# The setup of a gated cross-attention kernel: constant matmuls during the first loads, a smaller first load, another order of keys, queries and mask words

## The reference, cut to what matters

```python
x = x + tanh(g_xattn[0]) * xattn(layernorm(x), ctx_1024, mask, Wq, Wk, Wv, Wo)   # 2048 rows of 256
x = x + tanh(g_ffn[0])   * ffn(layernorm(x), Wg, W1, W2, W3)                     # 8 experts, 2 for each row

def xattn(inputs_q, inputs_kv, mask, Wq, Wk, Wv, Wo):        # 16 heads of 64, 1601 keys
    q = inputs_q @ Wq; k = inputs_kv @ Wk; v = inputs_kv @ Wv
    scores = einsum('bthd,bThd->bhtT', q, k) / sqrt(64)
    scores = where(mask, scores, finfo(float32).min)
    return (softmax(scores) @ v) @ Wo
```

## Time and profile before

| | |
|---|---|
| median of 3 runs | 627.38 us (626.77 to 627.91) |
| profiled execution | 626.95 us, span 625.1 us, so 1.85 us lie around the span |
| TensorE (PE) matmul busy | 590.8 us, 95% |
| VectorE (DVE) busy | 406.8 us, 65% |
| GpSimd (POOL) busy | 309.0 us, 49% |
| ScalarE (ACT) busy | 272.5 us, 44% |
| mean granted TensorE clock | 0.990 of full speed |

### The profile page before, as it was taken

The page is one execution under the profiler, slowest core; times in us unless marked ns, Lnnn a source line. Parts: engine busy times, 40 slices in busy tenths (PEclk is TensorE's granted clock), DMA queues, the critical chain, the costliest instruction groups (busy, mean ns, idle before and its releaser), DMA issues.

```text
span 625.1 us, 10907 instructions
## 1 busy us (share of the span) xinstructions
PE 590.8 (95%) x2882; PEld 343.7 (55%) x2883; DVE 406.8 (65%) x1266; ACT 272.5 (44%) x713; POOL 309.0 (49%) x272
## 2 busy tenths in 40 slices
PE   3899999999999999999999999889999999999993
PEld 2444465555556555555655555446666656666562
DVE  3578978898998989988899976247353222322231
ACT  2765665566565665665655554212412221122210
POOL 3643554565564698565796655412463222222221
PEclk9999999999999999999999989989999999999998
DMA  8944577586777889687686866999576442333312
GB/s 312 328 111 105 115 163 165 126 183 151 165 148 176 170 191 209 131 181 175 162 205 146 176 150 152 285 323 282 117 165 118 66 57 42 49 51 52 46 23 26
DMA packets 113970, 93.72 MB, mean 150 GB/s; under 512 B 38513, under 2 KB 107505, under 8 KB 113905
## 3 DMA queue, kind: packets, MB, share of 16 engines
q1 hardware_dynamic: 91824, 70.37, 46.5%
q10 hardware_dynamic: 15360, 13.64, 9.9%
q0 software_dynamic: 6720, 8.95, 8.5%
HBM read 27.72 MB, written 12.36 MB: 64 GB/s over the span
## 4 chain that ended last, share of the span: by engine, by line
PE 71%; DVE 13%; issue 4%; ACT 3%; DMA 3%; SPq 3%; ACTq 1%; POOLq 0%; POOL 0%; DVEq 0%
PE ps_s L1625 20%; PE ps_o L1439 12%; PE ps_o L1653 9%; PE ps_s L1393 9%; DVE blocksT L1128 5%; PE ps_a L1449 5%; DVE probs L1116 4%; PE ps_t L1336 4%; PE ps_t L1646 2%; PE ps_o L1406 2%; DMA mask<-mask_dram 2%; ACT probs L720 2%; PE ps_t L1393 2%; PE ps_a L1336 1%; SPq L414 1%
## 5 line engine op out<-in xcount | busy, mean ns | idle before, releaser
L595 POOL TENSOR_TENSOR probs<-probs,inv_sum 128x802 f32<-128x802 f32 x128 | 195.2, 1526 | 138.4 <-DVE inv_sum L1105 137.3
L720 ACT ACTIVATE probs<-probs,neg_max 128x401 f32<-128x401 f32 x256 | 159.4, 625 | 107.3 <-DVE neg_max L1116 105.8
L1625 PE MATMUL ps_s<-w_sb,xgT 128*128 x288 | 137.0, 599 | 3.3 <-issue 3.3
L1116 DVE CUSTOM_DVE_ANT_0 probs<-ps_s,biases 128x401 f32<-128x401 f32 x215 | 116.2, 571 | 21.2 <-PE ps_s L1393 14.4
L1128 DVE STREAM_TRANSPOSE blocksT<-probs 128x832 f32<-128x832 f32 x124 | 129.0, 1040 | 0.4 <-POOL probs L595 0.4
L646 POOL DMA_INDIRECT out_dram<-yg,ids x36 | 56.1, 1559 | 147.3 <-DVE yg L1286 136.8
L1439 PE MATMUL ps_o<-probsT,v_sb 128*64 128x512 f32 x496 | 113.6, 600 | 0.0
L1393 PE MATMUL ps_s<-kT,qT 64*128 64x201 f32 (+1 forms) x860 | 109.6, 350 | 3.5 <-DVE neg_max L1116 2.8
L1393 PEld LDWEIGHTS ps_s<-kT,qT 64*128 64x128 f32 x860 | 84.9, 188 | 44.1 <-issue 27.2
L858 ACT COPY gatedT<-ps_t 128x512 f32<-128x512 f32 x36 | 21.1, 586 | 150.7 <-PE ps_t L1646 150.7
L1276 DVE TENSOR_TENSOR gated<-ps_s,silu 128x512 f32<-128x512 f32 x36 | 24.9, 691 | 91.9 <-PE ps_s L1625 87.5
(11 more groups left out here) (167 smaller groups left out, 515.7 us busy)
## 6 DMA issues: line engine op xcount, KB each, us to landing
probsT<-blocksT SPq DMA_DIRECT2D x276, 96.0 KB
probsT<-blocksT SPq DMA_DIRECT2D x92, 128.0 KB
probsT<-blocksT ACTq DMA_DIRECT2D x96, 96.0 KB
xg_blocks<-x_regrouped SPq DMA_DIRECT2D x156, 32.0 KB, 2.1
probsT<-blocksT ACTq DMA_DIRECT2D x32, 128.0 KB
w_sb<-W1T_dram SPq DMA_DIRECT2D x8, 512.0 KB, 5.1
w_sb<-W2T_dram SPq DMA_DIRECT2D x8, 512.0 KB, 6.2
w_sb<-W3T_dram SPq DMA_DIRECT2D x8, 512.0 KB, 8.0
```

The lines of the kernel that those rows point to most:

```text
L595: pool.tensor_tensor(duo, duo, inv_sum[:, u:u + 2].unsqueeze(2).to_broadcast([P, 2, LASTK]), ALU.mult)\
L720: act.activation(probs[:, b, 0:LASTK], probs[:, b, 0:LASTK], ACT.Exp, bias=neg_max[:, b:b + 1], scale=-1.0, accum_out=sum_exp[:, b:b + 1]) ...
L1116: dve.tensor_tensor_reduce(probs[:, b, 0:LASTK], scores_bank(u)[:, 0:LASTK], biases[:, tile, :], HD ** -0.5, 3e38, ALU.add, ALU.min, neg_m ...
L1625: mm = pe.matmul(bank[:, :], xgT[:, buf, k, :], w_sb[:, bass.ds(expert, 1), (n * KT + k) * FH:(n * KT + k + 1) * FH].squeeze(1), start=(k ...
```

## The change

- TensorE starts with 16 matmuls of the constant `ones` (128x128) with itself into `ps_o` (`WARM = 16`), whose result nothing reads. GpSimd fills `ones` first of all, and TensorE waits for that alone before them.
- The first load of Wk has the columns of head pairs 0 and 1 (256 of 1024) instead of 512; those of pairs 2 and 3 come as a load of their own (`wk0_in`) behind the first half of Wq and ahead of mask part 0.
- TensorE makes the two transposes between `keys(0)` and `keys(1)`, and `keys(2)` right behind `queries(0)` instead of in step 0. `keys(0)` and `keys(1)` go into `ps_s2` and `ps_s3`; `scores(0)` waits for `keys(0)` alone, `scores(1)` for both.
- ScalarE follows that order, with `mask_words(0)` ahead of the copy of `queries(0)`, and `keys(2)` behind it.
- Part 1 of the mask words (`WORDS_DVE = (1,)`) is reduced by VectorE with a maximum over 1200 words, behind its own small reduction of the same part, and counts on a semaphore of its own (`words_of`).

The diff, with pieces that only carry semaphore counts left out:

```diff
@@ -68,8 +68,10 @@
 SCHED_TILES = {2: (1, range(0, 12)), 3: (1, range(12, 24)), 7: (2, range(0, 11)), 8: (2, range(11, 22))}
 SCHED_STEP = 103
 LAST_DUO = DUOS - GT
+WARM = 16
+WORDS_DVE = (1,)
 PRE = 6
-K_STEPS = {0: 2, 6: 3, 7: 4, 8: 5, 10: 6, 12: 7}
+K_STEPS = {6: 3, 7: 4, 8: 5, 10: 6, 12: 7}
 BURST = 24
 QUERIES_T = HP
 XN_STEP = 20
@@ -210,10 +212,10 @@
 
         x_in, w_in, g_in = [sem(f"x{g}_in") for g in range(NR)], [sem("w0_in"), sem("w1_in")], sem("g_in")
         wo_in = sem("wo_in")
-        kv_in, wk1_in, wv_in = sem("kv_in"), sem("wk1_in"), sem("wv_in")
+        kv_in, wk0_in, wk1_in, wv_in = sem("kv_in"), sem("wk0_in"), sem("wk1_in"), sem("wv_in")
         mask_in = [sem(f"mask{c}_in") for c in range(MASK_DMAS)]
         mask_pad, biases_ready = sem("mask_pad"), sem("biases_ready")
-        words_seen, mask_seen = sem("words_seen"), sem("mask_seen")
+        words_seen, words_of, mask_seen = sem("words_seen"), sem("words_of"), sem("mask_seen")
         const_ready, pads_ready = sem("const_ready"), sem("pads_ready")
         ln_stat, ln = sem("ln_stat"), sem("ln")
         std_ready, xn_ready = sem("std_ready"), sem("xn_ready")
@@ -369,8 +373,9 @@
                 sp.dma_start(xs[:, GT * g:GT * g + GT, :], x[g * GQ:(g + 1) * GQ, :].rearrange("(t p) d -> p t d", p=P))\
                   .then_inc(x_in[g], 16)
 
-            def load_half(w_tile, w, half, done):
-                c0, c1 = half * H * HD // 2, (half + 1) * H * HD // 2
+            def load_part(w_tile, w, c0, c1, done):
+
+                c0, c1 = c0 * P, c1 * P
                 sp.dma_start(w_tile[:, :, c0:c1], w[:, c0:c1].rearrange("(k p) n -> p k n", p=P)).then_inc(done, 16)
 
             def load_mask(c):
@@ -379,17 +384,18 @@
 
             load_x(0)
             sp.dma_start(ctx_last[:, :, 0:LASTK], ctxT[:, LAST0:].rearrange("(k p) n -> p k n", p=P)).then_inc(kv_in, 16)
-            load_half(wk_sb, Wk, 0, kv_in)
-            load_half(wq_sb, Wq, 0, w_in[0])
+            load_part(wk_sb, Wk, 0, 2, kv_in)
+            load_part(wq_sb, Wq, 0, 4, w_in[0])
+            load_part(wk_sb, Wk, 2, 4, wk0_in)
             sp.wait_ge(mask_pad, 1)
             load_mask(0)
             sp.dma_start(wv_sb[:, :, :], Wv.rearrange("(k p) n -> p k n", p=P)).then_inc(wv_in, 16)
             for c in range(1, MASK_DMAS):
                 load_mask(c)
-            load_half(wk_sb, Wk, 1, wk1_in)
+            load_part(wk_sb, Wk, 4, 8, wk1_in)
             for g in range(1, NR):
                 load_x(g)
-            load_half(wq_sb, Wq, 1, w_in[1])
+            load_part(wq_sb, Wq, 4, 8, w_in[1])
             sp.dma_start(gates[:, 0:1], g_xattn.partition_broadcast(P)).then_inc(g_in, 16)
             sp.dma_start(gates[:, 1:2], g_ffn.partition_broadcast(P)).then_inc(g_in, 16)
             sp.dma_start(wo_sb[:, :, :], Wo.rearrange("(k p) n -> p k n", p=P)).then_inc(wo_in, 16)
@@ -505,9 +511,10 @@
 
         @block.gpsimd
         def _(pool):
+            pool.memset(ones[:, :], 1.0).then_inc(const_ready, 1)
             pool.memset(mask8[:, :, SKP - 4:], 0).then_inc(mask_pad, 1)
             pool.memset(ident[:, :], 0.0).then_inc(const_ready, 1)
-            pool.wait_ge(const_ready, 1)
+            pool.wait_ge(const_ready, 2)
             pool.affine_select(out=ident[:, :], in_=ident[:, :], compare_op=ALU.not_equal, fill=1.0, base=0,
                                pattern=[[-1, P]], channel_multiplier=1).then_inc(const_ready, 1)
             pool.memset(probs[:, :, LASTK:], 0.0).then_inc(pads_set, 1)
@@ -515,7 +522,6 @@
             pool.memset(both[:, 0:GT, :], 0.0).then_inc(pads_ready, 1)
             pool.memset(used[:, :], 0.0).then_inc(pads_ready, 1)
             pool.memset(used_rows[:, :], 0.0).then_inc(pads_ready, 1)
-            pool.memset(ones[:, :], 1.0).then_inc(const_ready, 1)
             pool.memset(pads[:, :], 0.0).then_inc(pads_made, 1)
             pool.memset(before[:, :], 1.0).then_inc(const_ready, 1)
             pool.wait_ge(const_ready, 4)
@@ -677,7 +684,7 @@
 
             def keys(p):
                 act.wait_ge(k_ps, p + 1)
-                act.mul(kT[:, p, :], (ps_s[p] if p < 2 else ps_t[p % 2])[:, 0:LASTK], -1.0).then_inc(k_ready, 1)
+                act.mul(kT[:, p, :], (ps_s[2 + p] if p < 2 else ps_t[p % 2])[:, 0:LASTK], -1.0).then_inc(k_ready, 1)
 
             def queries(c):
                 act.wait_ge(q_ps, c + 1)
@@ -691,7 +698,7 @@
 
                 act.wait_ge(mask_in[c], 16)
                 if c >= 1:
-                    act.wait_ge(words_seen, c)
+                    act.wait_ge(words_seen, len([b for b in range(c) if b not in WORDS_DVE]))
                 words = mask8[:, c * MT:(c + 1) * MT, :].bitcast(I32)
                 act.activation(blocksT[:, 1, 0:5, :, :].rearrange("p c u n -> p (c u n)")[:, 0:MT * LAST0 // 4]
                                .rearrange("p (t n) -> p t n", t=MT), words[:, :, 0:LAST0 // 4], ACT.Copy,
@@ -768,7 +775,7 @@
                     exps(n)
                 if n % 4 == 0 and QUERIES_T < n // 4 + 2 <= CHUNKS:
                     queries(n // 4 + 1)
-                if n + 1 < MASK_DMAS:
+                if n + 1 < MASK_DMAS and n + 1 not in WORDS_DVE:
                     mask_words(n + 1)
                 if n % 4 in (2, 3) and 0 <= (n - 6) // 4 < CHUNKS - 1:
 
@@ -784,11 +791,12 @@
                             regroup(act, c, g, b)
 
             keys(0)
-            keys(1)
             move_xnT(0)
             move_xnT(1)
+            keys(1)
+            mask_words(0)
             queries(0)
-            mask_words(0)
+            keys(2)
             for n in range(PRE):
                 step_of(n)
 
@@ -922,6 +930,10 @@
                 words = mask8[:, c * MT:(c + 1) * MT, :].bitcast(I32)
                 dve.tensor_reduce(word_max[:, 1, c * MT:(c + 1) * MT], words[:, :, LAST0 // 4:], AX.X, ALU.max)\
                    .then_inc(mask_seen, 1)
+                if c in WORDS_DVE:
+
+                    dve.tensor_reduce(word_max[:, 0, c:c + 1], words[:, :, 0:LAST0 // 4], AX.XY, ALU.max)\
+                       .then_inc(words_of, 1)
 
             statistics(0, GT)
             mean_and_rsqrt(0, GT, 0)
@@ -931,7 +943,8 @@
 
             def mask_flag():
                 dve.wait_ge(mask_seen, MASK_DMAS)
-                dve.wait_ge(words_seen, MASK_DMAS)
+                dve.wait_ge(words_seen, MASK_DMAS - len(WORDS_DVE))
+                dve.wait_ge(words_of, len(WORDS_DVE))
                 dve.tensor_reduce(rowflag[:, 0:1], word_max[:, 0, 0:MASK_DMAS], AX.X, ALU.max).then_inc(flag_step, 1)
                 dve.tensor_reduce(rowflag[:, 1:2], word_max[:, 1, :], AX.X, ALU.min).then_inc(flag_step, 1)
                 dve.wait_ge(flag_step, 2)
@@ -1319,6 +1332,10 @@
 
         @block.tensor
         def _(pe):
+            pe.wait_ge(const_ready, 1)
+            for n in range(WARM):
+
+                pe.matmul(ps_o[:, 0:P], ones[:, :], ones[:, :], start=True, stop=True)
             pe.wait_ge(const_ready, CONSTS)
             pe.wait_ge(kv_in, CTX_WK)
 
@@ -1326,7 +1343,7 @@
                 if p >= 4:
                     pe.wait_ge(k_ready, p - 1)
                 for k in range(KT):
-                    mm = pe.matmul((ps_s[p] if p < 2 else ps_t[p % 2])[:, 0:LASTK], wk_sb[:, k, p * P:(p + 1) * P],
+                    mm = pe.matmul((ps_s[2 + p] if p < 2 else ps_t[p % 2])[:, 0:LASTK], wk_sb[:, k, p * P:(p + 1) * P],
                                    ctx_last[:, k, 0:LASTK], start=(k == 0), stop=(k == KT - 1))
                 mm.then_inc(k_ps, 1)
 
@@ -1382,7 +1399,10 @@
                 if t == 0:
                     pe.wait_ge(q_ready, c + 1)
                     if c < HP:
-                        pe.wait_ge(k_ready, max(2, c + 1))
+                        pe.wait_ge(k_ready, c + 1)
+                if d == 1:
+
+                    pe.wait_ge(k_ready, 2)
                 if d == BURST + 2:
                     pe.wait_ge(xnT_ready, 2 * NR)
                 if d >= 2:
@@ -1521,12 +1541,14 @@
                     routing(r, s)
 
             keys(0)
-            keys(1)
             transpose_xn(0)
             transpose_xn(1)
+            keys(1)
             pe.wait_ge(w_in[0], 16)
             pe.wait_ge(xnT_ready, 2)
             queries(0)
+            pe.wait_ge(wk0_in, 16)
+            keys(2)
             for n in range(PRE):
                 step_of(n)
 
```

7 lines of the change are left out of this document (5 added, 2 removed).

## The result

The changed kernel took **631.06 us** (median of 20 runs, 627.73 to 634.61) against 627.52 for the kernel before beside it (20 runs, 625.99 to 630.49): ratio **1.0036, 95% interval 1.0019 to 1.0053**. It is slower by 0.36%; the forecast was 625.7, with a range to 627.6. The profiled execution took 631.35 us, its span 628.1, so 3.2 us lie around the span, where it was 1.85.

What follows compares the result with a forecast made beforehand. Loads and waits between engines bound the setup, TensorE the rest; `values(1)` at 26.47 instead of 28.17 saves 1.7 us, which from the median 627.38 gives 625.7 us, range 623.9 to 627.6.

Steps and rivals of the forecast that it cites:

- Warm-ups: Start of TensorE: 16 constant matmuls hide behind the loads, so `keys(0)` runs at full clock; the slow start cost 1.1 us.
- first load: Start of the keys: 256 KB of Wk instead of 512 lets them start 0.7 us sooner, at 8.34.
- order: TensorE's setup: the new order, with `keys(2)` filling the wait for the queries' copy, puts `scores(0)` at 15.74, not 17.70.
- words 0: ScalarE's setup: mask words 0 ahead of `queries(0)` take 1.2 us and are hidden, ScalarE being free at about 14.3.
- Words 1 on VectorE: VectorE's setup: the long reduction takes 1.45 us and ScalarE waits for it; words left in place would give 0.7 more.
- The clock in the new pause: Rival, TensorE before `values(1)`: a 3.4 us pause drops the clock, costing 1.7 us; 627.4, no change; chance 0.22.
- the 1.7 us reach the end: Whole kernel: `values(1)` at 26.47 instead of 28.17 shortens the profiled execution from 626.95 to 625.25.
- nothing hangs on the setup: Behind `values(1)`: only mask parts and x groups hang on the setup, and they landed before they were wanted.
- something that might go away: Rival, clock falls at 370.27 and 407.82: if one no longer comes, 1.7 us more are gained, 624.0; chance 0.10.
- The slower rival: TensorE's start: the clock falls before `keys(0)`, half clock to some 15.2, 3.4 us lost, 629.1; chance 0.06.
- the signs of being wrong: Clock 0.50 before 30 us; first key matmul at 9.0; `scores(0)` early but `values(1)` not; shift at 28 gone behind 370.

Runs made afterwards that it cites:

- `words_on_scalar`: The changed kernel with part 1 of the mask words put back on ScalarE; 627.12 us, ratio 1.0004 to the kernel before.
- `before_look_a`: The kernel before, unedited, profiled once more in a single execution; 627.24 us.
- `before_words_dve`: The kernel before with only part 1 of the mask words moved to VectorE; 627.38 us, ratio 0.9997.
- `hold_expert_1`: The changed kernel with SyncE holding the second expert's weights until the last product of probabilities and values; 629.79 us, ratio 1.0030 to the kernel before.
- `before_warmups`: The kernel before with only the 16 constant matmuls at the start added; 626.56 us, ratio 0.998.
- `warm_12`: The changed kernel with 12 constant matmuls at the start instead of 16; 627.41 us, ratio 0.9997 to the kernel before.
- `order_and_load`: The changed kernel without the constant matmuls and without mask words on VectorE; 627.63 us, ratio 0.9998 to the kernel before.
- `no_warmups`: The changed kernel without the 16 constant matmuls at its start; 630.3 us, ratio 1.0044 to the kernel before.

## Why the prediction was wrong

*Warm-ups, first load, order, words 0: right*, and better than said: `scores(0)` at 15.27 for 15.74; the keys start 1.6 us sooner, not 0.7, and wait that out for the normalised x. The smaller load can't be credited with it: with the old load they start at 9.04, 7.91 and 7.56 in the three profiles of the kernel before, and `values(1)` stands at 28.17, 28.36 and 28.17. There an early landing won nothing, and the forecast's 0.7 us were read from a single landing. *Words 1 on VectorE: right* (1.39 for 1.45; ScalarE idle 1.51 us; 0.4 us of cost by `words_on_scalar` for 0.7).

*The clock in the new pause: right as a mechanism, wrong in its chance.* I put 0.22 on it, with the argument that a pause of 3.4 us need not bring a fall. In this case's profiles it does in 8 of 10. Its price by the traces is 1.4 to 1.65 us, near the 1.7 forecast. With the chance put right, the forecast would have stood at about 627, no change.

*The step that failed* is "the 1.7 us reach the end. The profiled execution took 626.95, which becomes 625.25". It takes two terms for fixed, without a reason for either: the time at half clock in the rest of the kernel, and the 1.85 us around the span. Measured over all executions, the changed kernel has 5.7 us more at half clock, 2.8 us at half price, and 3.3 us around the span instead of 1.8, 1.5 more. Less the 2.0 us that are left of the setup's gain, this is the +2.4 of the means (the medians, with most of its executions in the upper group, differ by 3.5). The sentence ahead of it, that nothing hangs on the setup, was right in what it says of the 330 us behind `values(2)`: the lead stays at 0.75 to 0.80 us from 33 to 364 us.

The forecast read one profile of the kernel before and one window of 100 us for all that comes behind the setup, from 100 to 200 us, which it calls late. Behind 364 us the executions part. At 386 us TensorE waits for ScalarE, in the profile after:

```profile
386.43 1.97 PE L1469 MATMUL ps_a<-wo_sb,oT 128*128 128x256 f32 x8 [2.53 <-ACT counts L721]
```

The same wait was 1.17 us in the profile before and 1.41 in `before_look_a`, which shows no fall at 370 either; against that profile, 0.9 us of lead at 257 us is 0.2 us of lag here. In this execution ScalarE is late because of its own queue. Its last two issues of `probsT<-blocksT` take 2.42 us instead of 1.28 (timelines of ScalarE, before, then after):

```profile
384.27 1.28 ACTq L357 DMA_DIRECT2D probsT<-blocksT  x2
```

```profile
382.05 2.42 ACTq L361 DMA_DIRECT2D probsT<-blocksT  x2
```

In the other three profiles of the changed kernel the wait is 1.85, 1.39 and 1.18 us, so this point does not take the lead away as a rule. From there to the first feed-forward matmul all hangs on a chain of issues by SyncE with waits between them, whose length differs from execution to execution with the stall and with where the falls of the clock come. In the four profiles of the changed kernel the falls ahead of the last matmul last 6.8 to 17 us in all, in the three of the kernel before 3.4 to 6.8. Rows 9 held the warning: two falls and a pause of 3.4 us stand there, and I priced them only as something that might go away. No rival had them come more often or last longer. I also wrote that both falls stand right behind pauses; ahead of the one at 370.27 TensorE was idle for no more than 1.37 us.

*The slower rival* (half clock until 15 us) did not occur. Of the signs of being wrong, two came: a granted clock of 0.50 before 30 us, and in the profile after a lead that is there at 28 us and gone behind 370.

What is **shown**: the setup's gain; the fall behind the pause, its price, and that filling the pause removes it; that the changed kernel's executions differ by their time at half clock; and the time outside. What is **open**: what brings the late stall, what sets the time outside the span, and why the clock falls more often behind 360 us in some versions than in others. Whether the stall brings falls or the falls the stall was not tried. The fall in the setup is not all of it: it stands in all four profiles of the changed kernel and so makes up 3.4 of the 5.7 us more at half clock.

## What to carry to other kernels

Follow a lead won early to each point where another engine or a queue ends a wait, and read more than one profile of the kernel before to see how much these points move by themselves. A lead can be kept in full and still not show in the time: put the mean granted clock and the time outside the span of every execution beside its time, and compare those first. When work is brought forward on TensorE and what it waits for next is not, the pause grows: write down its new length beside the pauses that have a fall behind them, and fill it with constant matmuls if it comes near (here this saved a fall of 3.4 us at half clock, worth 1.4 to 1.65 us, and cost nothing). A change of one microsecond in a kernel whose executions lie in two groups 4 us apart needs its median of many runs, and its parts tried alone.

## What the runs showed of the hardware that was not expected

- The time of an execution less its span depends on the program, on one chip as on another: 1.7 to 1.9 us in 126 executions of the kernel before and in 12 of `before_words_dve`; 2.05 to 2.25 in 96 executions of eight versions, longer and shorter programs among them; 2.3 to 4.6, with medians of 3.0 to 3.3, in 58 of the changed kernel, `words_on_scalar` and `hold_expert_1`, all with 16 constants at the start and no others. `before_warmups`, with the same 16 constants, shows both: 1.7 to 2.1 in eight executions, 2.9 to 3.2 in four. `warm_12` differs from the changed kernel in four matmuls and has 2.1.
- Idle times of 2.17 us (`warm_12`, before the keys), 2.85 us (`order_and_load`) and 2.86 us (`words_on_scalar`) brought a granted clock of 0.50 just behind them, while 3.29 us in `no_warmups` and `hold_expert_1` did not.
- Near 400 us ScalarE and VectorE stand still 4.4 and 2.6 us beyond the end of the matmuls that they read (397.15 and 399.08 in the profile after), and go on within 0.15 us of SyncE's next issue, while GpSimd goes on (its issues of L592 at 397.77 and 399.04 in the profile after) and the DMA engines move 363 GB/s:

```profile
398.70:402.46 3.76, 0.38 (x3) 0.00 (x1) 0.81 (x2) 0.58 (x1) 0.99 (x2) 0.91 1.07 363
```
